# Feed-forward phases of a macaron block: the exponent mask as a tensor operand

## The reference

```python
x = x + 0.5 * ffn(layernorm(x), w_gate, w_up, w_down)
x = x + attention(layernorm(x), Wq, Wk, Wv, Wo, We)      # 16 heads over 4096 tokens
x = x + 0.5 * ffn(layernorm(x), w_gate, w_up, w_down)

def fp4_linear(x, w):                                     # both operands quantized first
    return einsum('bsk,nk->bsn', quant(x), quant(w))
def ffn(x, w_gate, w_up, w_down):                         # 256 -> 704 -> 256
    h = silu(fp4_linear(x, w_gate)) * fp4_linear(x, w_up)
    return fp4_linear(h, w_down)
```

## Time and profile before

| | |
|---|---|
| time, median of 3 executions | 4101.06 us (4098.67 to 4104.31) |
| the profiled execution | 4091.76 us |
| its span, first to last instruction | 4090.0 us |
| first feed-forward phase, in the trace | about 84 to 346 us |
| second feed-forward phase | about 3815 to 4090 us |
| granted TensorE clock, whole span | 0.968 |

### The profile page before, as it was taken

One profiled execution on the slowest core, in us unless ns is written; L12 is line 12 of the kernel. 1 busy time (PEld: TensorE's weight loads), 2 busy tenths in 40 slices (PEclk: granted clock), 3 DMA queues, 4 the chain that ended last, 5 costly groups with the idle time before them and its releaser, 6 DMA issues. The chain is left out here.

```text
span 4090.0 us, 91456 instructions
## 1 busy us (share of the span) xinstructions
PE 3806.7 (93%) x29214; PEld 2212.5 (54%) x29214; DVE 3301.8 (81%) x5171; ACT 2483.3 (61%) x2892; POOL 472.8 (12%) x272
## 2 busy tenths in 40 slices
PE   1997599999999999999999999999999999995698
PEld 1786445555554555555555555555555555553587
DVE  7995488888888888788888888888888888885797
ACT  2663256666666666666666666666666666663464
POOL 3882100000000000000000000000000000000487
PEclk6998799999999999999999999999999999997899
DMA  3002611212122122212121212121212121213200
GB/s 122 1 0 84 160 35 36 44 37 45 36 47 41 41 40 42 44 36 44 36 44 38 44 39 44 38 44 36 44 36 45 38 45 37 47 38 92 69 18 20
DMA packets 316656, 186.52 MB, mean 46 GB/s; under 512 B 195447, under 2 KB 246551, under 8 KB 315831
## 3 DMA queue, kind: packets, MB, share of 16 engines
q1 hardware_dynamic: 316342, 182.35, 20.1%
HBM read 147.75 MB, written 33.82 MB: 44 GB/s over the span
## 5 line engine op out<-in xcount | busy, mean ns | idle before, releaser
L1164 DVE TENSOR_REDUCE tops<-coarse 128x1 f32<-128x512 f32 x4144 | 2681.3, 686 | 578.6 <-PE coarse L1025 475.2
L1140 ACT ACTIVATE probs<-fine 128x1024 f32<-128x1024 f32 x2048 | 1998.5, 1022 | 1014.9 <-PE fine L1044 1014.8
L1055 PE MATMUL o_ps<-probs,vh 128*32 128x512 f32 x8192 | 1088.9, 604 | 0.2 <-ACT probs L1140 0.2
L1034 PE MATMUL fine<-query_a,key_a 64*128 64x512 f32 x4096 | 921.1, 446 | 23.1 <-issue 19.6
L1034 PEld LDWEIGHTS fine<-query_a,key_a 64*128 64x128 f32 x4096 | 386.4, 185 | 929.1 <-ACT probs L1140 750.6
L1025 PE MATMUL coarse<-key_a,max_query 64*128 64x512 f32 x4144 | 832.6, 397 | 43.2 <-DMA key_c<-scratch_c_key 22.3
L1044 PE MATMUL fine<-query_b,key_b 33*128 33x512 f32 x4096 | 816.5, 394 | 0.0
L1040 PE MATMUL fine<-query_c,key_c 64*128 64x512 f32 x4096 | 814.5, 393 | 0.0
L1025 PEld LDWEIGHTS coarse<-key_a,max_query 64*128 64x128 f32 x4144 | 394.2, 186 | 113.5 <-DVE tops L1164 30.0
L1044 PEld LDWEIGHTS fine<-query_b,key_b 33*128 33x128 f32 x4096 | 388.9, 185 | 88.8
L1040 PEld LDWEIGHTS fine<-query_c,key_c 64*128 64x128 f32 x4096 | 389.3, 186 | 82.9
(11 more groups left out here) (158 smaller groups left out, 2377.3 us busy)
## 6 DMA issues: line engine op xcount, KB each, us to landing
query_c<-scratch_c_query SPq DMA_DIRECT2D x258, 128.0 KB, 2.6
max_query<-scratch_q_hi SPq DMA_DIRECT2D x524, 32.0 KB, 1.8
max_query<-scratch_c_query SPq DMA_DIRECT2D x262, 64.0 KB, 2.0
query_a<-scratch_q_hi SPq DMA_DIRECT2D x516, 32.0 KB, 1.8
query_a<-scratch_c_query SPq DMA_DIRECT2D x258, 64.0 KB, 2.0
query_b<-neg_max SPq DMA_DIRECT2D x1032, 0.5 KB, 2.0
query_b<-scratch_q_lo SPq DMA_DIRECT2D x258, 32.0 KB, 2.4
scratch_attended<-result SPq DMA_DIRECT2D x512, 8.0 KB
```

The costliest lines, as they stand in the source:

```text
L1034: pe.matmul(fine[i % 2][:, r, :], key_a[kp][half_rows(r, 0, HALF), cols], query_a[half][half_rows(r, 0, HALF), :], start=True, stop=False)
L1055: last = pe.matmul(o_ps[32 * j:32 * (j + 1), :], vh[kp][:, kt, :], probs[:, kt // 2 % RING, kt % 2, :], start=g == 0, stop=g == NG - 1)
L1140: act.activation(probs[:, i % RING, :, :], fine[i % 2][:, :, :], ACT.Exp).then_inc(probs_ready, 1)
L1164: dve.tensor_reduce(tops[n][:, idx // KB, idx % KB:idx % KB + 1], bank[:, :], AX.X, ALU.max).then_inc(tops_ready, 1)
```

## The change

The mask is written once for each phase, as an int32 word in each partition, into the last word of the PSUM bank `small_ps`, by a memset on VectorE that VectorE then waits for. L496, an operation of one tensor and a constant, becomes an operation of two tensors: the second operand is that one PSUM word, read again for every element. All else stays.

```diff
+        exponent = small_ps[:, 511:512].bitcast(I32)
...
+        mask_ready = sm("mask_ready")
...
                 dve.tensor_scalar(tmp, mean, -1.0, None, ALU.mult).then_inc(centre_ready, 1)
+                dve.memset(exponent, 0x7F800000).then_inc(mask_ready, 1)
+                dve.wait_ge(mask_ready, 1)
                 chain = Chain(dve, joint_chain)
...
-                    dve.tensor_scalar(step[n][:, cols].bitcast(I32), xn[n][:, cols].bitcast(I32), 0x7F800000, None, ALU.bitwise_and).then_inc(power_ready, 1)
+                    dve.tensor_tensor(step[n][:, cols].bitcast(I32), xn[n][:, cols].bitcast(I32), exponent.to_broadcast([P, (hi - lo) * BLK]),
+                                      ALU.bitwise_and).then_inc(power_ready, 1)
```

## The result

The changed kernel takes 4068.74 us (median of 6 executions, 4067.72 to 4074.49), the kernel before 4101.02 us (6 executions, 4091.66 to 4104.52). The ratio is 0.9924, 95% interval 0.9912 to 0.9936: 0.76% faster, some 31 us (the interval is 26 to 36 us), where 29 us and 4072 us were forecast.

The account below looks back on a forecast made before the run. The prediction took a 7.47 us loop through GpSimd, closed by L496's wait, to bound the feed-forward rounds. Gains of 14.0 and 15.0 us, plus 0.8, less at most 0.9, net 29 us: 4072 us, range 4064 to 4086.

Parts of the forecast that it names:

- The wait inside L496: Feed-forward rounds: about 1 us of each L496 is waiting for GpSimd's L421, ending 0.52 us after it; the change removes it.
- The price of the new L496: The two-tensor AND on VectorE takes 1.15 us for 960 numbers, against 0.66 us for the free old one.
- The next bound, first phase: First feed-forward phase: rounds fall from 7.47 to 6.91 us, set by VectorE and ScalarE; 25 rounds give 14.0 us.
- The next bound, second phase: Second feed-forward phase: rounds fall from 7.47 to 6.87 us, set by TensorE; 25 rounds give 15.0 us.
- GpSimd's late last pass: L426 after L421: its 0.22 us late start and 1.99 us duration come from L496; 1.83 us, back to back, afterwards.
- The ends of the phases: Outside the 25 rounds: round 28 gains about 0.4 us a phase; narrow instructions lose at most 0.9 us together.
- The sum: Whole kernel: both phases' rounds and the ends net 29 us less, 4101.06 to 4072 us.
- The wait that stays: Rival for the feed-forward rounds: the new L496 still waits, ending 1.01 us after L421; 7.96 us rounds, 4126 us; chance 0.06.
- The slow AND: Rival for the new L496: the AND of a repeated word takes 2.30 us, 4127 us in all; chance 0.05.
- TensorE's shortfall: Rival: `gate_up` starts only behind the last transpose's end, 7.12 us a round; gain 17 us, 4084 us; chance 0.11.
- nothing comes of it: Rival: instruction turned back into the old form, or gain lost in unseen waits; 4101 us; chance 0.04.

Follow-up runs that it names:

- the extra pass: Changed kernel with one more AND of 256 columns into a spare tile ahead of each row's AND: 4083.47 us, ratio 0.9966 to the kernel before.
- the moved reciprocal: Changed kernel with the reciprocal of the block scales moved ahead of `h_lo` in VectorE's order: 4070.39 us, ratio 0.9931 to the kernel before.

## Why the prediction was right

The time, 4068.74 us, lies in the forecast's range, and the mechanism is the one that it named. The timed gain, 26 to 36 us, could not tell 29 from 31 us; the traces give the terms, and there errors of up to 1.1 us cancel in part. What follows goes step by step.

- **The wait inside L496.** Right. Two experiments move it as said, in opposite directions: with GpSimd's passes cut short it takes 0.68 us, and with the slower instruction, the mask in SBUF, it ends 1.01 us behind the pass's end, where 1.01 was worked out for the rival.
- **The price of the new L496.** 1.15 us forecast from L494 and L720, 1154 ns measured.
- **The next bound, first phase.** 6.91 us forecast, 6.912 measured; the loop is VectorE's and ScalarE's, as the extra pass (0.33 us a round) and the moved reciprocal (0.09 us off) show. The term is 13.9 us, forecast 14.0.
- **The next bound, second phase.** TensorE, as forecast, but 6.85 us in its steady rounds where 6.87 was forecast, and 6.822 on average over the 25, since rounds 3 to 11 take 6.78, near the 6.77 that was worked out for VectorE's and ScalarE's loop. The term is 16.1 us, forecast 15.0.
- **GpSimd's late last pass.** Wrong, without a share in the sum. The prediction put both the 0.22 us ahead of L426 and its longer duration down to L496, and named "back to back with L421" as a sign of being right. The duration fell, 1963 to 1832 ns on average, but the idle time stayed: 12.1 us for the 56 in both kernels, and 0.23 us even where GpSimd's passes are 16 columns long and no AND is near. What it comes from is not shown; it is not the AND. So GpSimd's loop without the wait is 6.67 us (2.34 + 2.50 + 1.83, from the rows above), not 6.53; it stays below the other two.
- **The ends of the phases.** Round 28 and what follows gave 0.47 us in the first phase and took 0.17 in the second, where 0.4 in each was forecast. The start of the first phase gave 1.6 us that was not in the sum at all; it is not the change's (last section). Ahead of the loop more was lost than the 0.13 us of the sum: from VectorE's last preparing pass to `x_lo` it is 10.35 us before (83.67 to 94.02) and 10.59 after (83.63 to 94.22), 0.24 us, and about as much in the second phase. Of this 0.07 us lies ahead of the first row of maxima, which starts 0.03 us after ScalarE's pass ends before (84.94 to 84.97) and 0.10 us after it in the changed kernel (84.90 to 85.00), though the memset (83.82 to 83.88) falls well into the wait that was to cover it; why is not shown. Behind the last `hidden` 0.1 and 0.2 us were lost, where at most 0.34 a phase was allowed.
- **The sum.** 13.9 + 16.1 us in the rounds, 0.3 behind round 28, less 0.5 ahead of the loops and 0.3 behind them, is 29.5 us, forecast 28.9. The second phase was taken 1.1 us too low and the ends 0.5 us too high. The 31.9 us of the table hold the 1.6 us of chance on top, so their agreement with the timed gain to within a microsecond is partly luck.
- **The rivals.** The wait that stays came true for the mask in SBUF: 4126 us was its price, 4130 us its time, and 1.01 us behind the pass's end was worked out and measured. Its rounds took 7.99 us where 7.96 was worked out; over the kernel before on its own chip it lost 32.6 us, not 25. In the changed kernel it is excluded by L500's 1.15 us inside L423. The slow AND is excluded by the same row. TensorE's shortfall is excluded by the floor of 6.85 us, and that nothing comes of it by the interval of the ratio.

The Trainium skill's rule on the double-rate form ("VectorE: DVE Perf Modes", section "The perf-mode tier table") held with 0.68 against 1.15 us. What it says of the time shows where GpSimd is out of the way: there the change is worth nothing, 4066.21 against 4067.05 us. The 0.47 us in each AND that it costs show in no timed difference, because TensorE holds most rounds; in the traces the first phase's rounds are 0.09 us longer with the new AND (6.91 against 6.82). The Trainium skill's page "SBUF — State Buffer", section "SBUF: two separate sides", names two SBUF inputs beside the double-rate form as what takes the shared ports; the experiment with the mask in SBUF agrees.

## What to carry to other kernels

Where VectorE and GpSimd work at once, look for VectorE instructions that last longer than the same shape elsewhere and end a fixed time after a GpSimd pass: the wait hides in the duration, not in the idle time. A constant or a small operand moved to PSUM and streamed as a tensor frees such an instruction, at the price of the single rate; a scalar there, or a tensor in SBUF, does not. Before the gain is counted, add up the loops that come next: here they stood 0.56 and 0.64 us a round away, and it was they that set what the change was worth.

## What the runs showed of the hardware beyond this

The first three rounds of a phase take 18.64, 20.2 or 21.75 us, in steps of 1.56 us, and which of them differs from one profile to another and between the phases of one: 20.2 in both phases before; 18.64 and 20.19 after; 21.7 in both with the mask in SBUF. Each step is a round in which `gate_up` runs in part at the lower clock: in the ten profiles 23 of the 60 first rounds are such, and in each of them seven or eight of its matmuls start 0.43 us apart, in the other 37 none. TensorE's timeline in the changed kernel's second phase, and the windows around such a round and around the same place of the first phase, both 6.32 us behind the first `hidden` (the granted clock, PEclk, is the third figure from the right):

```profile
3834.67 0.50 PE L176 MATMUL g_ps<-gu_hi,xt_hi 128*128 128x512 f32 x1 [1.89 <-DVE xt_lo L452]
...
3835.77 0.63 PE L176 MATMUL g_ps<-gu_hi,xt_hi 128*128 128x512 f32 x1
...
3838.89 0.39 PE L178 MATMUL g_ps<-gu_hi,xt_lo 128*128 128x512 f32 x1
```
```profile
core 0: us, PE busy (x) PEld busy (x) DVE busy (x) ACT busy (x) POOL busy (x), PEclk, DMA share, GB/s
3833.50:3841.50 8.00, 5.87 (x20) 4.64 (x20) 5.60 (x8) 4.26 (x8) 5.52 (x3) 0.79 0.00 1
107.24:115.24 8.00, 4.94 (x23) 4.04 (x24) 7.15 (x10) 5.78 (x9) 5.51 (x3) 1.00 0.00 1
```

The matmuls start 0.43 us apart there (3835.77 to 3836.20 for the next) and 0.23 us at full clock (3838.89 to 3839.12), the levels of 1.2 and 2.4 GHz; the 0.79 of the window mixes the two. Ahead of it TensorE had waited 1.89 us for `x_lo`, as in every one of the 60 first rounds (1.88 or 1.89 us), so that wait alone doesn't tell in which the clock falls. So a difference of 1.6 us in the start of a phase between two profiles of this kernel says nothing about the change, and of the 31.9 us above 1.6 are of that kind. Why it falls in one and not in the next was not tried and stays open.
